# Output projection of an attention block: softmax sums loaded with repeated rows and inverted on 128 partitions, in place of flat reciprocals spread by matmuls

## The reference

```
attn = jax.nn.softmax(attn + bias, axis=-1)
out = jnp.einsum('bqk,bkd->bqd', attn, v)
out = out.reshape(B, nh, H, W, hd).transpose(0, 2, 3, 1, 4).reshape(B, H, W, C)
return out @ proj_w + proj_b
...
x = x + _L0_conv_ref(_ln_c(x), ...)
t = _to_tokens(x)
t = t + _L0_ffn_ref(_ln_t(t), ...)
```

## Time and profile before

| | us |
|---|---|
| median of three runs | 2328.25 |
| lowest and highest of the runs | 2328.11, 2330.27 |
| the profiled execution's own time | 2332.33 |
| span of its trace, first to last instruction | 2330.6 |
| phase_proj in the trace, first issue to the last sum of rows | 1522.3 to 1584.2 |
| mean granted TensorE clock over the span | 0.929 |

### The profile page before, as it was taken

The page is one execution under the profiler, slowest core; times in us unless marked ns, Lnnn a source line. Parts: engine busy times, 40 slices in busy tenths (PEclk is TensorE's granted clock), DMA queues, the critical chain, the costliest instruction groups (busy, mean ns, idle before and its releaser), DMA issues. The chain is left out here.

```text
span 2330.6 us, 38125 instructions
## 1 busy us (share of the span) xinstructions
PE 2061.9 (88%) x12356; PEld 1882.0 (81%) x12356; DVE 1783.8 (77%) x3335; ACT 1661.2 (71%) x2909; POOL 756.0 (32%) x523
## 2 busy tenths in 40 slices
PE   6933347999999999999999999965799999999997
PEld 6922226888888888888888888744799999999997
DVE  5654446999999999999999998556677777777774
ACT  3344405888888888888888888912577778877785
POOL 0030031445444554445454445530122211221121
PEclk9955577999999999999999999977799999999999
DMA  6778893465544655546555454132566766777774
GB/s 208 223 164 188 189 168 72 85 127 101 105 95 77 125 106 101 103 76 116 107 101 113 78 106 79 57 122 93 170 212 215 223 216 215 220 219 226 214 211 115
DMA packets 123366, 334.59 MB, mean 144 GB/s; under 512 B 17648, under 2 KB 56008, under 8 KB 117860
## 3 DMA queue, kind: packets, MB, share of 16 engines
q1 hardware_dynamic: 111888, 312.42, 54.2%
q0 software_dynamic: 10400, 19.87, 3.9%
q10 hardware_dynamic: 960, 0.80, 0.1%
HBM read 269.62 MB, written 63.43 MB: 143 GB/s over the span
## 5 line engine op out<-in xcount | busy, mean ns | idle before, releaser
L891 DVE TENSOR_REDUCE mx<-ps_m 128x1 f32<-128x384 f32 x1212 | 643.4, 553 | 102.4 <-PE ps_m L746 96.8
L842 ACT ACTIVATE p_hi<-ps_s 128x768 fp32r<-128x768 f32 x648 | 528.2, 815 | 138.8 <-PE ps_s L760 135.3
L595 POOL TENSOR_TENSOR p_lo<-p_f,p_hi 128x768 fp32r<-128x768 f32 x216 | 398.8, 1846 | 614.9 <-ACT p_f L848 614.9
L848 ACT ACTIVATE p_f<-ps_s 128x768 f32<-128x768 f32 x648 | 525.1, 810 | 1.3 <-POOL p_lo L595 1.3
L746 PE MATMUL ps_m<-key_hi,query_hi 128*128 128x384 f32 x1240 | 418.2, 344 | 49.6 <-DMA query_hi<-rel_hi_d 40.2
L595 DVE TENSOR_TENSOR p_lo<-p_f,p_hi 128x768 fp32r<-128x768 f32 x432 | 417.0, 965 | 38.8 <-ACT p_f L848 37.9
L1580 ACT CAST w_hi<-w_raw 128x384 fp32r<-128x384 f32 x600 | 290.2, 516 | 135.8 <-PE ps_o L1557 130.3
L1698 DVE TENSOR_TENSOR w_lo<-w_raw,w_hi 128x384 fp32r<-128x384 f32 x600 | 316.5, 556 | 79.0 <-ACT w_hi L1580 78.9
L757 PE MATMUL ps_s<-query_hi,key_hi 128*128 128x384 f32 x1296 | 338.7, 342 | 12.5 <-DMA query_rest<-m_d 10.4
L770 PE MATMUL ps_o<-p_hi,val 128*65 128x384 f32 x1296 | 331.7, 337 | 1.8 <-POOL p_lo L595 1.6
L760 PE MATMUL ps_s<-query_rest,key_rest 121*128 121x384 f32 x1296 | 332.2, 338 | 0.0
(11 more groups left out here) (209 smaller groups left out, 2927.8 us busy)
## 6 DMA issues: line engine op xcount, KB each, us to landing
w_raw<-w_u SPq DMA_DIRECT2D x200, 576.0 KB, 4.6
query_rest<-rel_lo_d SPq DMA_DIRECT2D x36, 864.0 KB
query_rest<-qk_lo_d SPq DMA_DIRECT2D x36, 576.0 KB
query_rest<-qk_hi_d SPq DMA_DIRECT2D x36, 576.0 KB
rel_lo_d<-out_lo SPq DMA_DIRECT2D x6, 1728.0 KB, 30.6
query_hi<-rel_hi_d SPq DMA_DIRECT2D x12, 864.0 KB, 18.5
v_d<-v_sb SPq DMA_DIRECT2D x6, 1170.0 KB, 7.5
val<-v_d SPq DMA_DIRECT2D x12, 585.0 KB, 7.3
```

Of the source, the lines that this page charges most:

```text
L595: engine.tensor_tensor(p_lo[r][:], p_f[idx % 2], p_hi[r][:].bitcast(F32), ALU.subtract).then_inc(lo_done(0, idx)[0], 1)
L842: act.activation(p_hi[r][:], ps_s[:, bank:bank + 2, 0:TB], ACT.Exp).then_inc(hi_ok, 1)
L848: act.activation(p_f[idx % 2], ps_s[:, bank:bank + 2, 0:TB], ACT.Exp).then_inc(f_ok, 1)
L891: dve.tensor_reduce(mx[s // TILES][:, s // 3 % 6, col:col + 1], ps_m[:, c, 0:TB], AX.X, ALU.max).then_inc(mx_ok, 1)
```

## The change

The flat load, its reciprocal, the way over rec_d, the matrix `spread`, its matmuls and the PSUM tensor ps_r go. In their place sums_d is loaded six times three times (one load for each block and each part c) with each head's row repeated on 32 partitions, into a buffer rec of 128 x 3 x 2304. VectorE inverts a block's 128 x 3 x 384 in place inside normalised, waits for itself, and multiplies SBUF by SBUF. VectorE's loop is written out as a Python loop, TensorE's runs over all blocks.

```
-            sp.dma_start(rflat[:], sums_d.rearrange("h n -> (h n)").rearrange("(p n) -> p n", p=P)).then_inc(s_in, 16)
+            def load_sums(b):
+                cols = slice(b * TB, (b + 1) * TB)
+                for c in range(KC):
+                    sp.dma_start(rec[:, c, cols],
+                                 sums_d[c * HPT:(c + 1) * HPT, cols].rearrange("h (a n) -> h a n", a=1).broadcast_to([HPT, HD, TB])).then_inc(rec_in[b], 16)
+
+            load_sums(0)
             rows = OALL_HEADS * HD - (KC - 1) * P
             sp.dma_start(o_all[rows:P, KC - 1, :], o_d[OALL_HEADS * HD:C, :]).then_inc(o_in, 16)
 
-            sp.wait_ge(r_ok, 1)
-            sp.dma_start(rec_d.rearrange("h n -> (h n)").rearrange("(p n) -> p n", p=P), rflat[:]).then_inc(rec_out, 16)
-            sp.wait_ge(rec_out, 16)
-            sp.dma_start(rsum[:], rec_d).then_inc(rec_in, 16)
             for g in range(X_LOADS):
                 rows = slice(g * TILES // X_LOADS, (g + 1) * TILES // X_LOADS)
+                load_sums(2 * g + 1)
+                if g + 1 < X_LOADS:
+                    load_sums(2 * g + 2)
                 sp.dma_start(x1[:, rows, :], x.rearrange("(t p) c -> p t c", p=P)[:, rows, :]).then_inc(x_in[g], 16)
...
-            pe.wait_ge(spread_made, 3)
-            pe.wait_ge(rec_in, 16)
             pe.wait_ge(w_lo_ok, 1)
-            spread_block(0)
-            with pe.Fori(0, BLOCKS // 2 - 1) as i:
+            with pe.Fori(0, BLOCKS // 2) as i:
                 for par in range(2):
-                    spread_block(2 * i + par + 1)
                     product(2 * i + par, par)
-            spread_block(BLOCKS - 1)
-            product(BLOCKS - 2, 0)
-            product(BLOCKS - 1, 1)
...
             def normalised(blk, par):
-                dve.wait_ge(spread_ok, blk + 1)
-                dve.tensor_tensor(o_f[par][:], ps_r[:, :, 0:TB], o_all[:, :, bass.ds(blk * TB, TB)], ALU.mult).then_inc(of_ok, 1)
+                cols = slice(blk * TB, (blk + 1) * TB)
+                dve.wait_ge(rec_in[blk], 16 * KC)
+                dve.reciprocal(rec[:, :, cols], rec[:, :, cols]).then_inc(rec_ok, 1)
+                dve.wait_ge(rec_ok, blk + 1)
+                dve.tensor_tensor(o_f[par][:], rec[:, :, cols], o_all[:, :, cols], ALU.mult).then_inc(of_ok, 1)
                 dve.wait_ge(ohi_ok, blk + 1)
                 dve.tensor_tensor(o_lo[par][:], o_f[par][:], o_hi[par][:].bitcast(F32), ALU.subtract).then_inc(olo_ok, 1)
 
...
-            dve.wait_ge(s_in, 16)
-            dve.reciprocal(rflat[:], rflat[:]).then_inc(r_ok, 1)
             dve.wait_ge(w_hi_ok, 1)
             dve.tensor_tensor(w_lo[:], w_raw[:], w_hi[:].bitcast(F32), ALU.subtract).then_inc(w_lo_ok, 1)
             dve.wait_ge(o_in, 16)
             normalised(0, 0)
-            with dve.Fori(0, BLOCKS // 2 - 1) as i:
-                for par in range(2):
-                    normalised(2 * i + par + 1, 1 - par)
-                    added(2 * i + par)
-                    measured(2 * i + par)
-            normalised(BLOCKS - 1, 1)
-            for blk in (BLOCKS - 2, BLOCKS - 1):
+            for blk in range(BLOCKS):
+                if blk + 1 < BLOCKS:
+                    normalised(blk + 1, (blk + 1) % 2)
                 added(blk)
                 measured(blk)
```

More of the change, by code:

```diff
@@ L947, with phase_proj @@
 ROW = C + EXPERTS
-def phase_proj(nc, x, o_d, sums_d, rec_d, proj_w, proj_b, out, o_all, x1, stats):
+def phase_proj(nc, x, o_d, sums_d, proj_w, proj_b, out, o_all, x1, stats):
     with ExitStack() as ctx:
@@ L961, in sem @@
             return ctx.enter_context(nc.semaphore(name))
[L963 to L966, removed]
+        rec = sb("rec", [P, KC, S])
         o_f = [sb(f"o_f{i}", [P, KC, TB]) for i in range(2)]
@@ L973, in phase_proj @@
         p_b = sb("p_b", [P, C])
-        ps_r = ctx.enter_context(nc.psum_tensor("ps_r", [P, KC, 512], F32))
         ps_y = ctx.enter_context(nc.psum_tensor("ps_y2", [P, TPB, 512], F32))
-        s_in = sem("sums_in")
-        rec_out = sem("rec_out")
-        rec_in = sem("rec_in")
+        rec_in = [sem(f"rec_in{b}") for b in range(BLOCKS)]
+        rec_ok = sem("rec_ok")
         o_in = sem("o_in")
@@ L983, in phase_proj @@
         w_in = sem("w_in2")
-        spread_made = sem("spread_made")
         w_hi_ok = sem("w_hi_ok2")
@@ L987, in phase_proj @@
         x_ok = sem("x_ok")
-        r_ok = sem("r_ok")
-        spread_ok = sem("spread_ok")
         of_ok = sem("of_ok")
@@ L1018, in _ @@
         def _(pool):
[L1019 to L1027, removed]
             pool.wait_ge(w_in, 32)
@@ L1037, in _ @@
         def _(pe):
[L1038 to L1044, removed]
             def product(blk, par):
@@ L1771, in program @@
     sums_d = dram("sums_d", [HEADS, S])
-    rec_d = dram("rec_d", [HEADS, S])
     xn_d = dram("xn_d", [S, C + EXPERTS])
@@ L1786, in program @@
             stats = tokens.enter_context(nc.sbuf_tensor("x1_stats", [P, TILES, 6], F32))
-            phase_proj(nc, x, o_d, sums_d, rec_d, proj_w, proj_b, out, room[:, 0:KC, :], x1, stats)
+            phase_proj(nc, x, o_d, sums_d, proj_w, proj_b, out, room[:, 0:KC, :], x1, stats)
             xt_hi = room[:, 0:KC, :].bitcast(F32R)
```

## The result

The changed kernel takes 2373.68 us (median of four runs, 2372.39 to 2374.68); the kernel before, in the same comparison, 2329.26 (2328.11 to 2331.24). The ratio is 1.019, interval 1.0172 to 1.0207: slower by 44.4 us. The forecast was 38.2 us and 2366.5 us, the range 2360 to 2379.

A forecast was written before the change was run, and what follows sets the result against it. TensorE and VectorE's chain were taken as about equally the bound of phase_proj. Summed from 1534.0: 68.0 + 11.6 + 1.2 + 7.0 + 0.56 = 1622.4, minus 1584.2: 38.2 us longer, 2366.5 us, range 2360 to 2379.

The forecast's parts named there:

- The reciprocals: Six 128 x 1152 reciprocals in VectorE's chain in phase_proj, 7.35 us each, paid whole.
- C: Rival: a long-row reciprocal on VectorE costs one pass, 1.36 us, giving 2330.5 us, no measurable change; chance 0.04.
- E: Rival: VectorE's reciprocal takes eight passes a column, 10.9 us each, +21 us, 2388 us; chance 0.03.
- upper bound of 8.02: Highest time allowed for one VectorE reciprocal, in us, scaling the 216-column row whole to 1152 columns.
- The start, 1534.0: Time in phase_proj, in us, when VectorE's first reciprocal starts, bounds 1532.5 and 1536.4.
- bound of 1536.4: Latest landing of o_d, in us, if sums loads ahead of it use four DMA engines, 5.9 us a block.
- GpSimd's additions: Bias additions stretch VectorE's two-operand SBUF instructions; one taken, 1.2 us, bounds none and 4.2 us.
- D: Rival: GpSimd stretches VectorE's reciprocals by about 2, +7 to +15 us, 2374 to 2381 us; chance 0.05.
- The last product: TensorE's final product at phase_proj's end: 6.9 us, bounds 5.0 and 9.1, plus 0.1 for the handover.
- The rest of the chain: VectorE's other work per block: multiplication 1.36, cast 1.23, then 1.36, addition and statistics 2.91 us; period 14.2 us.
- The loads behind the first block: Later loads of sums and x rows in phase_proj come in time and cost nothing.
- rival B: Loads become the bound: a broadcast load on one DMA engine, 23.6 us a block, +110, about 2438 us; chance 0.04.

The follow-up runs named there:

- e2: Changed kernel with only the first 192 of 384 columns of each part inverted; 2354.38 us.
- e1: Changed kernel without the six reciprocals, multiplying by the sums themselves; 2341.71 us, ratio 1.0056 to the kernel before.
- e7: e4 with the flat 216-column reciprocal and rec_d back, loads repeating rec_d's rows, no reciprocal in VectorE's chain; 2339.49 us, ratio 1.0044 to the kernel before.
- e4: Changed kernel with the sums loaded by one load for each head, 72 loads in place of 18; 2366.5 us.
- e3: Changed kernel with the load of o_all's last rows issued ahead of the first sums; 2371.74 us.
- e6: Changed kernel without GpSimd's additions of the bias to x, bias left out of the result; 2370.72 us.
- e5: Changed kernel with 48 unused matmuls ahead of each product's wait, keeping TensorE busy; 2371.77 us.
- e9: e8 with the first x rows loaded before the wait for the flat reciprocals' store; 2332.43 us, ratio 1.001 to the kernel before.
- e10: e9 without GpSimd's bias additions, bias left out of the result; 2321.74 us, ratio 0.9981 to the kernel before.
- e8: e7 with 36 loads in place of 72, some from ScalarE's queue, x rows earlier; 2331.7 us, ratio 1.0006 to the kernel before.
- e11: e9 with the bias added by an fp32 matmul on TensorE in place of GpSimd's additions; 2335.8 us, ratio 1.0027 to the kernel before.
- e12: Kernel before with the bias added by an fp32 matmul in place of GpSimd's additions; 2352.61 us, ratio 1.0094.

## Why the prediction was right

- **The reciprocals.** 7.34 us each against 7.35, on the path whole. e2 confirms the slope (6.25 ns a column); e1, and e7 against e4, confirm that they were paid. Rivals C and E, and the upper bound of 8.02, are refuted by the row itself.
- **The start, 1534.0.** Mis-sized: with the phase's start 0.25 us later it should have been 1534.3 and was 1537.8, 3.5 us more and 1.1 beyond the bound of 1536.4. The mechanism was the one named (o_d queued behind loads on few engines), but I took the middle between the bounds, arguing that the 7.0 us of o_all's load was measured beside other loads. It took 13.2. The bound itself was too low because it gave each of the four engines 25 GB/s; they moved 81 together, so a block of sums takes 7.3 us and not 5.9 (an estimate from that rate), 1.4 us more, which covers the 1.1. e3 (1.9 us by order alone) and e4 (4.5 us by loads by head) show that it was these loads.
- **GpSimd's additions.** Taken as one stretched instruction, 1.2 us; measured 3.1 (0.13 + 1.12 + 0.77 + 1.11), inside the bound of 4.2. e6 gives 3.1 in the phase. The x rows came later than before, so the additions fell on the second and third blocks, on two o_f and two o_lo. The reciprocals were not stretched (7.33 us beside additions), which refutes D.
- **The last product.** 8.0 us against 7.0, within the bounds. e5 shows 2.5 of it as the clock, for which the sum had 1.9; 0.5 is the wait for the PSUM bank, which my 0.1 us for the handover missed. The rows on record had it: o_lo ended at 1578.02 and the last product started at 1578.63.
- **The rest of the chain** was 0.1 us a block shorter than the sum, 14.14 against 14.24. With 3.5, 1.9 and 1.0 above it, this makes 38.2 into 44.1. The prediction called the 1.23 us for the cast VectorE's only regular gap before the change; its looped blocks also idled 0.3 us ahead of the statistics. The sum is not touched by this, since it took the addition and the statistics from code without a loop.
- **The loads behind the first block** cost nothing, as said, and rival B falls: the x rows landed in time because each block took 14 us. e1 shows what they would cost otherwise.

What I had priced too low is that the new multiplication is worse placed in another way: it reads the reciprocals from SBUF, not from PSUM. Beside GpSimd's additions this turns 1.36 us into up to 3.73 (e9, and e10 without them). The kernel before had its o_f at 1.36 there, between two o_lo that were held up:

```profile
1543.51 1.36 DVE L1086 TENSOR_TENSOR o_f<-ps_r,room 128x1152 f32<-128x1152 f32 x1 [1.00 <-PE ps_r L1042]
```

No run changed only the place of that operand, so this rests on the two traces. Of the variants with repeated loads none that computes all of the result beats the kernel before: e8 is level with it, and the matmuls of the kernel before, which look like overhead, also seem to keep the multiplication out of GpSimd's way.

## What to carry to other kernels

Count an elementwise operation by columns for each partition: inverting before repeating costs 216 columns, after repeating 6912, and these took 44.0 us, 6.4 ns a column. That this equals the whole 44.1 us is partly chance: the smaller gains and losses around them cancel. Look for the price of an unusual width on a line through the widths that the trace has. For a load whose outermost dimension is small, take the upper bound of its delay, also for what is queued behind it. And before a slow step is removed, look what it covers: loads or contention that were free beneath it come back.

## What the runs showed of the hardware

- A load with an outermost dimension of four heads kept about 0.27 of the DMA engines busy (81 to 87 GB/s), and the issuing engine was held up too, 2.4 us for a load of 192 KB once some were queued; by head, a load of 48 KB took 0.46 us to issue, and such loads alone moved 106 GB/s at a share of 0.42 (e4).
- A VectorE instruction with two SBUF operands beside GpSimd's additions took up to 3.74 us in place of 1.36 (e1; 3.73 in e9); reciprocals (7.33 to 7.35 us) and statistics (1.48 for three), with one SBUF operand, were not affected.
- An fp32 matmul with one row of weights and 384 columns took 0.84 us at full clock, as much as four to five of the fp32r matmuls (27 in 5.0 us); a tile with it took 2.61 us in place of 1.6 (e11).
- TensorE, busy throughout, stood at a mean granted clock of 0.58 for 21.3 us in e12. What kept it low stays open.
- The last product, started after 6.5 to 7.6 us of idling, took 6.9 to 8.0 us from the end of o_lo in four traces of the same matmuls (the changed kernel, e3, e4, e6), and 5.5 with TensorE kept busy before it (e5).
